# A ternary feed-forward: the multiply-and-add before rounding is done by ScalarE and not by VectorE

## The reference

```python
def _act_quant(x):
    scale = 127.0 / jnp.clip(jnp.max(jnp.abs(x), axis=-1, keepdims=True), 1e-05)
    xq = jnp.clip(jnp.round(x * scale), -128.0, 127.0) / scale
    return x + jax.lax.stop_gradient(xq - x)
def _bitlinear(x, w):
    return jnp.einsum('bsi,oi->bso', _act_quant(x), _weight_quant(w))
gate = jax.nn.silu(_bitlinear(x, w_gate))
up = _bitlinear(x, w_up)
return _bitlinear(gate * up, w_down)
```

## Time and profile before

| | us |
|---|---|
| median of 3 runs | 1066.5 |
| the profiled execution, its own time | 1070.84 |
| its span in the trace | 1069.0 |
| PE busy in the span | 991.3 (93%) |
| DVE busy | 543.5 (51%) |
| ACT busy | 434.3 (41%) |
| POOL busy | 267.3 (25%) |

### The profile page before, as it was taken

The page is one execution under the profiler, slowest core; times in us unless marked ns, Lnnn a source line. Parts: engine busy times, 40 slices in busy tenths (PEclk is TensorE's granted clock), DMA queues, the critical chain, the costliest instruction groups (busy, mean ns, idle before and its releaser), DMA issues.

```text
span 1069.0 us, 20661 instructions
## 1 busy us (share of the span) xinstructions
PE 991.3 (93%) x8414; PEld 715.4 (67%) x8423; DVE 543.5 (51%) x1357; ACT 434.3 (41%) x635; POOL 267.3 (25%) x406
## 2 busy tenths in 40 slices
PE   6978777999999988999999999999999999999997
PEld 4656544555467766676676476776667768999996
DVE  5588789985359999831531335884133144100000
ACT  5666555676455555542312325553221221221220
POOL 3022201101124434432312111675121002332211
PEclk9999989999999999999999999999999999999999
DMA  9700000000050100000000020003312136755500
GB/s 259 96 2 2 2 1 0 2 1 0 1 116 4 42 2 3 3 1 1 1 0 1 1 98 2 3 2 118 120 39 90 42 120 231 274 187 200 171 28 1
DMA packets 55359, 60.55 MB, mean 57 GB/s; under 512 B 23603, under 2 KB 47071, under 8 KB 55266
## 3 DMA queue, kind: packets, MB, share of 16 engines
q1 hardware_dynamic: 52322, 52.93, 16.6%
q0 software_dynamic: 2944, 6.30, 1.8%
HBM read 54.76 MB, written 7.21 MB: 58 GB/s over the span
## 4 chain that ended last, share of the span: by engine, by line
PE 66%; DVE 17%; ACT 2%; issue 2%; POOL 1%; DMA 1%; DVEq 0%; POOLq 0%; ACTq 0%
PE ps L1957 15%; PE ps L2262 10%; PE ps L2406 8%; PE ps L2419 7%; DVE small L851 6%; PE ps L2083 3%; PE ps L2340 3%; PE ps L1833 2%; PE ps L1794 2%; PE ps L1791 2%; PE ps L1869 2%; PE ps L1732 2%; PE ps L2085 1%; DVE small L956 1%; PE ps L1826 1%
## 5 line engine op out<-in xcount | busy, mean ns | idle before, releaser
L851 DVE TENSOR_REDUCE small<-ps 128x2 f32<-128x512 f32 (+2 forms) x176 | 149.3, 901 | 52.2 <-PE ps L1794 35.3
L1957 PE MATMUL ps<-r_w,r_k 128*128 128x256 f32 x512 | 113.2, 381 | 2.5 <-ACT r_k L1630 2.5
L2262 PE MATMUL ps<-r_a,r_w 128*128 128x512 f32 x256 | 112.0, 594 | 3.1 <-ACT r_a L1462 3.1
L1957 PEld LDWEIGHTS ps<-r_w,r_k 128*128 128x128 f32 x512 | 96.4, 190 | 18.6 <-issue 4.4
L1388 ACT ACTIVATE r_a<-ps 120x1024 f32<-120x1024 f32 (+1 forms) x80 | 77.5, 1021 | 62.1 <-PE ps L1841 62.0
L2262 PEld LDWEIGHTS ps<-r_a,r_w 128*128 128x128 f32 x256 | 48.2, 190 | 59.8 <-issue 56.0
L2406 PE MATMUL ps<-r_a,w_block 128*128 128x128 f32 x736 | 86.4, 275 | 1.0 <-ACT r_a L1694 0.7
L2406 PEld LDWEIGHTS ps<-r_a,w_block 128*128 128x128 f32 x736 | 85.6, 192 | 2.5 <-ACT r_a L1694 1.0
L1630 ACT ACTIVATE r_k<-ps,pvec 128x512 f32<-128x512 f32 x64 | 44.0, 687 | 101.0 <-PE ps L2262 101.0
L2419 PE MATMUL ps<-w_all,r_a 128*128 x368 | 83.2, 379 | 0.2 <-issue 0.2
L1702 ACT ACTIVATE r_a<-ps 128x512 f32<-128x512 f32 x46 | 27.5, 597 | 129.0 <-PE ps L2406 119.9
(11 more groups left out here) (277 smaller groups left out, 1802.9 us busy)
## 6 DMA issues: line engine op xcount, KB each, us to landing
w_block<-in_L_ffn_W SPq DMA_DIRECT2D x23, 1024.0 KB
w_all<-in_L_ffn_W SPq DMA_DIRECT2D x8, 1024.0 KB, 10.2
r_w<-in_L_xattn_a_li_w SPq DMA_DIRECT2D x4, 1024.0 KB, 7.2
x_rows<-x_all SPq DMA_DIRECT2D x4, 512.0 KB, 3.0
x_rows<-r_a SPq DMA_DIRECT2D x4, 512.0 KB, 3.0
x_all<-in_x SPq DMA_DIRECT2D x3, 512.0 KB, 6.5
y_all<-in_L_ffn_w_gate SPq DMA_DIRECT2D x1, 1024.0 KB, 9.0
y_all<-in_L_ffn_w_up SPq DMA_DIRECT2D x1, 1024.0 KB, 11.4
```

What stands on the lines that cost most here:

```text
L851: ins_ = dve.tensor_reduce(nm.rearrange("p (j s) -> p j s", j=4)[:, j:j + count, :], src, AX.X, ALU.max, negate=True)
L1957: ins_ = pe.matmul(o[:, t // 2, (t % 2) * D:(t % 2 + 1) * D], src[:, c, t * P:(t + 1) * P], w[:, c, :], start=(c == 0), stop=(c == chunks ...
L2262: ins_ = pe.matmul(o, LI[a]["li2"][:, c, m * P:(m + 1) * P], FT3[:, c, :], start=(c == 0), stop=(c == KC - 1))
```

## The change

DVE no longer multiplies the tile and adds `MAGIC`; it signals `hq_ready` behind the output scale. ACT does the multiply and add as one activation in place in `HH` (`Identity` with a scale per token and a bias), signals a new semaphore `hr_ready`, waits for it, and subtracts as before. Because ACT now reads the scale, it has two places in turns.

```diff
+        HIDDEN_SCALE = tuple(SC2 + k for k in range(2))
...
-                 "r_done", "r_ready", "dn_done", "y_ready", "cxh_ready", "cyT_done", "cyT_ready", "d_lid_ready",
+                 "r_done", "r_ready", "dn_done", "y_ready", "cxh_ready", "cyT_done", "cyT_ready", "d_lid_ready", "hr_ready",
...
                 def hidden_quant(p, i):
                     g = PT_TILES * p + i
                     dve.wait_ge(sem["hh_done"], 2 * g + 2)
-                    quant_scales(HH[g % 2], sa(AM2, 1), sa(SU2, 1), sa(SC2, 1))
-                    dve.tensor_scalar(sa(SD + i, 1), sa(SU2, 1), mean_w[:, 2:3], None, ALU.mult)
-                    dve.tensor_scalar(HH[g % 2], HH[g % 2], sa(SC2, 1), MAGIC, ALU.mult, ALU.add).then_inc(sem["hq_ready"], 1)
+                    quant_scales(HH[g % 2], sa(AM2, 1), sa(SU2, 1), sa(HIDDEN_SCALE[g % 2], 1))
+                    dve.tensor_scalar(sa(SD + i, 1), sa(SU2, 1), mean_w[:, 2:3], None, ALU.mult).then_inc(sem["hq_ready"], 1)
...
                 def whole(p, i):
                     g = PT_TILES * p + i
                     act.wait_ge(sem["hq_ready"], g + 1)
+                    act.activation(HH[g % 2], HH[g % 2], ACT.Identity, bias=magic[:], scale=sa(HIDDEN_SCALE[g % 2], 1)
+                                   ).then_inc(sem["hr_ready"], 1)
+                    act.wait_ge(sem["hr_ready"], g + 1)
                     act.activation(N2[g % 2], HH[g % 2], ACT.Identity, bias=neg_magic[:], scale=1.0).then_inc(sem["n2_ready"], 1)
```

## The result

The changed kernel took 1078.9, 1080.3 and 1082.3 us in its first timing, against 1066.5 us: ratio 1.013, 95% interval 1.0113 to 1.0146, so it is slower, by 13.8 us. (A fourth execution took 2571 us at full clock and is left out, as was one of 2038 us later; nothing here explains them.) The forecast was slower by 7.9 us, with a range that ended at 1079.5. The sign was right, the size was not, and 1080.3 lies 0.8 us above the end of the range. Two later timings of the same kernel gave 1.0106 (1.0089 to 1.0123) and 1.0092 (1.0076 to 1.0108). Over all three, its 13 runs lie between 1075.5 and 1082.3 us, with a median of 1077.6, 11 us above before.

What follows compares the result with a forecast made beforehand. DVE's queue and each tile's loop through ACT bound it early, PE from about 190 us, the loop touching it repeatedly. Delays of 6.7 + 0.6 + 0.6 = 7.9 us on 1066.5 gave 1074.4 us, range 1069.0 to 1079.5.

Steps and rivals of the forecast that it cites:

- the 0.84 us given back: Last input transposes (221.01): PE's 0.84 us wait for DVE's `front_quant(3)` goes, so the delay falls from 7.3 to 6.5.
- Steps 1 to 3: Tiles (0,0) to (0,3): ACT's later subtractions delay PE and DVE, +1.1, then +2.4, then +3.7 us at `silu(1,0,1)`.
- step 5: Tiles (1,1) to (2,2): late subtractions where transposes lack room raise the delay to 4.0, 5.4, 6.7, then 7.3 us.
- The unknown costs: Allowances outside the sum: self-wait +1.3, activation time -1.5 or +7.7, further low clock on PE nothing to +3 us.
- rival C: Worse than the sum: PE falls to low clock in more stretches, 7.9 + 4, giving 1078 to 1081; 13%.
- step 4: Up to the transposes at 177.78: DVE is the bound with one L998 fewer, 3.7 - 0.66 = +3.0 us.
- step 7: From 222 us: PE full, ACT has slack, nothing added to 250; then tiles (3,2) and (3,3) add 0.6 us each.
- Rival A: DVE sets the pace and gets its time back, 5 x 0.66 = 3.3 us before 177.78, giving 1063.2; 9%.
- Rival B: Hidden: PE, full from 190 us on, catches up the late subtractions; time 1066 to 1068; 9%.

Runs made afterwards that it cites:

- filled changed kernel: The changed kernel with 45 useless matmuls put into PE's queue where it waits; 1074.6 us, ratio 1.0074 to the kernel before.
- filled kernel before: The kernel before with the same 45 useless matmuls in the same places of PE's queue; ratio 0.9986 to the kernel before.
- third buffer: Changed kernel with three inner-tile buffers, so tile g's product waits for g-3's subtraction; ratio 1.0087 to the kernel before, 1.0053 with useless matmuls in PE's waits too.
- run with VectorE's work kept: Changed kernel where VectorE still runs a same-size instruction on other data (683 ns each) behind its signal; ratio 1.0118 to the kernel before.

## Why the prediction was right in sign and wrong in size

The table sets the sum against the delays that were measured at its own points, counted from the output scale of tile (0,0). "As it ran" is the second profile of the changed kernel minus the second of before. "Filled" is the filled changed kernel minus the filled kernel before; by the 0.43 us that the fillers cost the latter, it can be up to 0.4 too small.

| point | sum | as it ran | filled |
|---|---|---|---|
| transposes of the first pair (177.78) | 3.0 | 5.5 | 3.4 |
| tile (1,1) | 4.0 | 7.2 | 4.1 |
| tile (1,3) | 5.4 | 8.5 | 5.5 |
| tile (2,1) | 6.7 | 9.4 | 6.4 |
| tile (2,2) | 7.3 | 10.0 | 7.0 |
| last input transposes | 6.5 | 9.1 | 6.1 |
| tile (3,2) | 7.3 | 10.8 | 7.8 |
| tile (3,3) | 7.9 | 11.4 | 8.4 |

**Right.** The mechanism: a tile late by 1.24 + 0.03 us less 0.66, each of the places without room, the 0.84 us given back, nothing added behind the stage. Steps 1 to 3 hold to 0.1 us where neither clock nor fillers are in the way: the filled changed kernel against the run with tiles 4 to 15 changed has tile (0,1) 1.1 us late, (0,2) 2.4 and (0,3) 3.6, and the sum has 1.1, 2.4 and 3.7. In the table the sum is within about 0.5 us of the last column at every point. That is in part luck: two terms that it lacked, below, are offset there by the fillers' own 0.4 us and by step 5, which had 1.3 us from tile (1,3) to (2,1) where 0.9 were measured.

**Failed: the clock**, in "The unknown costs". The step said that further low stretches cost "nothing to +3", and the sum took nothing. They were 20.4 us in the stage against 10.2 before, and cost about 2.1 us net by the first pair's transposes and 3.0 by tile (1,1) (both up to 0.4 less, as above); behind that the two right-hand columns keep their distance. The reason I gave against rival C, that the added stops are single ones of 0.6 to 1.3 us, was wrong: the loop through pair 0 lengthens waits that were there already. PE's idle time ahead of the transposes of tile (0,2), at 155.13 in the changed kernel, went from 2.44 us to 3.61; in the second profile PE was busy 4.85 of 10 us in 150 to 160, and the clock was at 0.64 there. The row of before (PE's timeline of its first profile):

```profile
153.55 0.62 PE L2009 MATMUL ps<-identb,r_a 128*128 128x128 bf16 x8 [2.44 <-ACT r_a L1449]
```

In this stretch PE's own work lies in the loop. The fillers take 3.0 us off the changed kernel by tile (0,3) (22.99 to 19.97), and all of it is still there at the first pair's transposes (39.53 to 36.51). In the kernel before they take 1.7 us off by tile (0,3) and only 0.9 are left at those transposes, since VectorE sets the pace behind it. So the stop and the low clock are paid together.

**Failed: "DVE is the bound and has one L998 fewer"**, in step 4. DVE's delay did fall by 0.66 there (in the filled pair from 3.2 us at the second product of tile (1,0) to 2.5 at the next product), but then the product of tile (1,2) waits 0.87 us for the subtraction of tile (1,0) to free its buffer, and the delay is back at 3.4. I had followed the data of each tile to PE, and not the buffer back to DVE. The clean measure of the term is the 0.8 us that the third buffer gives in the filled kernels. The 3.4 in the table looks closer to the sum's 3.0 than it is, because its base is up to 0.4 us late by the fillers.

**Mis-sized: tile (3,2)**, in step 7: 0.6 in the sum, 1.2 as measured (from tile (3,1) to (3,2) the delay grows from 9.6 to 10.8 us, and in the filled kernels from 6.6 to 7.8). "ACT has slack" was true of PE's waits only. A `silu` that stands behind a new activation in ACT's queue reached DVE late, and DVE, which had no wait at this product before, carried that to this tile through its queue (timeline of DVE, before and changed):

```profile
234.66 1.44 DVE L990 SCALAR_TENSOR_TENSOR r_a<-ps,small,r_a 128x512 f32<-128x512 f32 x2
```

```profile
244.32 0.75 DVE L991 SCALAR_TENSOR_TENSOR r_a<-ps,small,r_a 128x512 f32<-128x512 f32 x1 [1.21 <-ACT r_a L1444]
...
248.60 0.72 DVE L991 SCALAR_TENSOR_TENSOR r_a<-ps,small,r_a 128x512 f32<-128x512 f32 x1
```

The run with VectorE's work kept is 0.6 us later still at this tile, so VectorE's queue does set it.

The rest, from 11.3 us in the stage to 13.8 in the first timing, lies within the spread of the runs and was in no step; what set it is not shown. Rival A holds only with the work gone (1062.6 us measured, 1063.2 said; part of the agreement is the place of the low clock). Rival B is refuted by PE's waits. Rival C, held at 13%, came nearest: its span of 1078 to 1081 holds the first timing's middle run, and the later timings lie just under it. The section of the Trainium skill on "Optimizing Scalar/DVE Operations" ("Perfetto Trace Analysis"), by which a saturated VectorE may hand work to ScalarE, would have given the wrong sign here (VectorE was busy 18.17 of 20 us from 150 to 170). Its sentence on bubbles caused by engines that aren't saturated names what the traces show: PE waits for ScalarE, 1.37 us at tile (1,3), though ScalarE is busy only 42% of the span. The remedy that it gives, smaller instructions, no run here tried.

## What to carry to other kernels

An engine that is busy half of the time can still be the place where the end is set, if it stands in a loop between two others. Before moving work onto it, follow one tile through the loop and ask at each hand-over how much room there is, in both directions: data forward, and buffers back. And when a change adds idle time to TensorE where its own work lies in that loop, price the matmuls behind the stop at half clock, since in this case that was 2.6 to 3.0 of 11.3 us; a run with useless matmuls in the waits tells that cost from the stop itself.

## What the runs showed of the hardware

- The place of the low stretches moves from run to run. Profiles whose kernels do the same work up to the transposes of tile (0,3) differed by 2 us there (16.3 against 18.4) because a stretch fell at another place. So a difference of 2 us in such a stage can't be read from one profile each; the time at half clock has to be read beside it.
- ScalarE can wait for its own last instruction at a cost of 0.03 us plus the lost overlap of about 0.1 us: 1.27 us from start to start for an instruction of 1.24, where the instruction behind a subtraction started 0.10 us before its end (243.13 against 242.08 + 1.15 in ACT's timeline of the changed kernel).
- 45 matmuls of no use made the kernel before 0.14% faster (0.01 to 0.26%), though at 0.23 us each (2.75 us for twelve) they are some 10 us of work; PE's busy time grew by 5.0 us (987.5 to 992.5), the rest of its work being done faster. The twelve ahead of tile (0,2)'s transposes, in PE's timeline of the filled changed kernel:

```profile
148.54 2.75 PE L2094 MATMUL ps<-r_k,identb 128*128 128x512 bf16 x12
...
152.42 0.62 PE L2012 MATMUL ps<-identb,r_a 128*128 128x128 bf16 x8 [1.13 <-ACT r_a L1452]
```

These twelve end 1.1 us before the transposes could start in the changed kernel and don't stand in their way. In the kernel before, the fillers together cost 0.43 us by tile (0,1), as shown above.
